# One value and one relative quarter of the products in each round; single maxima; first scores quad by quad

## The reference

```
Q, K, V = (layernorm(x) @ W.T + b) split into 16 heads of 8
rel_pos = arange(L)[None, :] - arange(L)[:, None] + 127      # clipped by the gather
scores  = einsum('bhld,bhrd->bhlr', Q, K) / sqrt(8) + einsum('bhld,lrd->bhlr', Q, relative_k[rel_pos])
attn    = softmax(scores)
out     = einsum('bhlr,bhrd->bhld', attn, V) + einsum('bhlr,lrd->bhld', attn, relative_v[rel_pos])
```

## Time and profile before

| | us |
|---|---|
| median of 3 runs | 2237.12 (2234.93 to 2237.24) |
| profiled execution, measured | 2237.36 |
| its span, first to last instruction | 2235.6 |
| PE busy | 2122.8 (95%) |
| DVE busy | 1701.9 (76%) |
| ACT busy | 1527.9 (68%) |
| POOL busy | 1059.3 (47%) |
| mean granted clock of TensorE | 0.991 |

### The profile page before, as it was taken

The page is one execution under the profiler, slowest core; times in us unless marked ns, Lnnn a source line. Parts: engine busy times, 40 slices in busy tenths (PEclk is TensorE's granted clock), DMA queues, the critical chain, the costliest instruction groups (busy, mean ns, idle before and its releaser), DMA issues.

```text
span 2235.6 us, 90813 instructions
## 1 busy us (share of the span) xinstructions
PE 2122.8 (95%) x37442; PEld 1549.0 (69%) x37442; DVE 1701.9 (76%) x3703; ACT 1527.9 (68%) x3290; POOL 1059.3 (47%) x992
## 2 busy tenths in 40 slices
PE   3999999999989999999899999999998999999998
PEld 1676766776667667676676676767776777777776
DVE  4788788888778888878688888788775676766675
ACT  3666666666666666666566666666664888888887
POOL 2443343344334433443343344434432777776776
PEclk8999999999999999999999999999998999999999
DMA  4112211321221122112212311222111222122110
GB/s 134 42 43 64 71 53 44 83 61 53 64 62 53 50 66 71 51 45 75 61 44 59 84 43 52 64 61 62 43 52 35 28 23 28 19 27 25 26 22 11
DMA packets 255701, 114.70 MB, mean 51 GB/s; under 512 B 142218, under 2 KB 251156, under 8 KB 255348
## 3 DMA queue, kind: packets, MB, share of 16 engines
q1 hardware_dynamic: 255348, 109.60, 20.2%
HBM read 83.34 MB, written 8.39 MB: 41 GB/s over the span
## 4 chain that ended last, share of the span: by engine, by line
PE 67%; DVE 12%; ACT 7%; issue 7%; POOL 3%; SPq 1%; DMA 0%; DVEq 0%; ACTq 0%; POOLq 0%
PE ps L1248 14%; PE ps L1187 9%; PE ps L1265 9%; PE ps L1194 7%; PE ps L1205 6%; PE ps L1277 5%; DVE neg_max L789 5%; POOL probs_t L500 3%; ACT probs L579 3%; ACT probs L646 2%; DVE probs_t L795 2%; PE ps L1431 2%; PE ps L1414 2%; PE ps L1416 2%; PE ps L1415 2%
## 5 line engine op out<-in xcount | busy, mean ns | idle before, releaser
L579 ACT ACTIVATE probs<-ps,neg_max 128x512 f32<-128x512 f32 x1024 | 695.0, 684 | 475.1 <-DVE neg_max L789 475.1
L789 DVE TENSOR_REDUCE neg_max<-ps 128x1 f32<-128x512 f32 (+1 forms) x768 | 619.5, 862 | 170.5 <-PE ps L1194 170.0
L439 POOL TENSOR_TENSOR stat_hi<-q_twice,mask8h 128x1024 f16<-128x1024 f16 x128 | 243.2, 1900 | 896.7 <-PE ps L1194 787.6
L1248 PE MATMUL ps<-const,probs 128*128 128x128 f32 x4096 | 516.3, 275 | 35.6 <-ACT probs L579 17.1
L1248 PEld LDWEIGHTS ps<-const,probs 128*128 128x128 f32 x4096 | 455.4, 142 | 89.1 <-issue 46.8
L795 DVE COPY probs_t<-ps 128x512 f32<-128x512 f32 x512 | 339.9, 685 | 88.7 <-PE ps L1248 84.5
L500 POOL TENSOR_TENSOR probs_t<-probs,probs_t 128x1024 f16<-128x1024 f32 x160 | 340.0, 2133 | 111.2 <-ACT probs_t L652 111.2
L568 ACT ACTIVATE probs_t<-ps 128x512 f32<-128x512 f32 x512 | 288.1, 596 | 98.2 <-PE ps L1248 94.7
L1187 PE MATMUL ps<-keys,stat_hi 128*32 128x512 f16 x4096 | 316.3, 384 | 1.8 <-issue 1.8
L1194 PE MATMUL ps<-rk_split,stat_rel 96*32 96x512 f16 (+1 forms) x4096 | 285.2, 353 | 0.0
L999 DVE SCALAR_TENSOR_TENSOR keys<-ps,comb,keys 128x128 f32<-128x128 f32 x640 | 179.8, 344 | 129.6 <-PE ps L1433 129.6
(11 more groups left out here) (136 smaller groups left out, 2870.2 us busy)
## 6 DMA issues: line engine op xcount, KB each, us to landing
rv_step<-in_rv_win SPq DMA_DIRECT2D x128, 512.0 KB, 3.9
keys<-keys SPq DMA_DIRECT2D x64, 96.0 KB, 2.2
x_pair<-in_x SPq DMA_DIRECT2D x8, 512.0 KB, 4.3
q_twice<-q_hi SPq DMA_DIRECT2D x32, 128.0 KB, 2.4
q_lo_pair<-q_lo SPq DMA_DIRECT2D x32, 128.0 KB, 2.8
rel_scratch<-rel_t SPq DMA_DIRECT2D x256, 16.0 KB, 3.2
x_pair<-in_x SPq DMA_DIRECT2D x16, 256.0 KB, 3.2
x_pair<-rel_scratch SPq DMA_DIRECT2D x64, 64.0 KB, 3.9
```

The lines of the kernel that those rows point to most:

```text
L579: nc.scalar.activation(probs[:, q, :], ps[:, i, :], ACT.Exp, bias=neg_max[:, q:q + 1], accum_out=row_sum[parity][:, s * QUADS + q:s * QUAD ...
L789: nc.vector.tensor_reduce(neg_max[:, IN_ROUND * j + at:IN_ROUND * j + at + n], ps[:, at:at + n, :], op=ALU.max, axis=AX_X, negate=True).th ...
L1248: last = nc.tensor.transpose(ps[:, bank, rt * P:(rt + 1) * P], probs[:, q, rt * P:(rt + 1) * P], ident)
```

## The change

Four things. Each of the four quads of a round gets its own reduce for the maximum, and every exponential waits for its own. In the steps 0 to 3, of the first two quads of each round, first terms and relative terms are issued quad by quad. Each round issues one batch of value products and one relative half, of step s - 2 (batch 1, half 1) in the first round and of step s - 1 (batch 0, half 0) in the second. The transposed relative rows go to the last quarter of the bank, and the wait for their copy (rel_t_ready) stands ahead of the value products of batch 1.

```diff
@@ -43,7 +43,6 @@
 
 ROUNDS = 2
 IN_ROUND = QUADS // ROUNDS
-MAXIMA = 3
 
 
 TR_BANKS = (0, 4, 5, 6)
@@ -574,8 +573,7 @@
                     act.wait_ge(tr_done, START + pair * TILES + (s - 1) * QUADS + IN_ROUND * (j + 1))
                 for i in range(IN_ROUND):
                     q = IN_ROUND * j + i
-                    if i < MAXIMA:
-                        act.wait_ge(max_done, START + ((pair * STEPS + s) * ROUNDS + j) * MAXIMA + i + 1)
+                    act.wait_ge(max_done, START + pair * TILES + s * QUADS + q + 1)
                     nc.scalar.activation(probs[:, q, :], ps[:, i, :], ACT.Exp, bias=neg_max[:, q:q + 1],
                                          accum_out=row_sum[parity][:, s * QUADS + q:s * QUADS + q + 1]).then_inc(exp_done, 1)
 
@@ -783,11 +781,10 @@
                                         rv_last_row[:].unsqueeze(1).broadcast_to([P, RT - FAR, D]), ALU.add).then_inc(operands_ready, 1)
 
             def maxima(pair, s, j):
-
-                for at, n in ((0, 1), (1, 1), (2, 2)):
-                    dve.wait_ge(score_done, START + pair * TILES + s * QUADS + IN_ROUND * j + at + n)
-                    nc.vector.tensor_reduce(neg_max[:, IN_ROUND * j + at:IN_ROUND * j + at + n], ps[:, at:at + n, :], op=ALU.max, axis=AX_X,
-                                            negate=True).then_inc(max_done, 1)
+                for i in range(IN_ROUND):
+                    q = IN_ROUND * j + i
+                    dve.wait_ge(score_done, START + pair * TILES + s * QUADS + q + 1)
+                    nc.vector.tensor_reduce(neg_max[:, q:q + 1], ps[:, i, :], op=ALU.max, axis=AX_X, negate=True).then_inc(max_done, 1)
 
             def evacuate(pair, s, q, piece):
 
@@ -824,7 +821,7 @@
                 dve.wait_ge(rel_tr, START + pair * STEPS + s + 1)
 
                 dve.wait_ge(rel_stored[s % 2], START + pair * STEPS * 16 + s // 2 * 32)
-                nc.vector.tensor_copy(rel_t[:, s % 2, :], ps[0:64, AV_BANK, 2 * P:3 * P]).then_inc(rel_t_ready, 1)
+                nc.vector.tensor_copy(rel_t[:, s % 2, :], ps[0:64, AV_BANK, 3 * P:4 * P]).then_inc(rel_t_ready, 1)
 
             def score_round(pair, parity, s, j, first, ahead):
                 maxima(pair, s, j)
@@ -1210,10 +1207,16 @@
                 for p in duos:
                     low_terms(parity, s, p)
                 for p in duos:
-                    for q in (2 * p, 2 * p + 1):
-                        first_terms(parity, s, q)
-                    for q in (2 * p, 2 * p + 1):
-                        relative_terms(s, q)
+                    if s < GROUP_STEPS and p % 2 == 0:
+
+                        for q in (2 * p, 2 * p + 1):
+                            first_terms(parity, s, q)
+                            relative_terms(s, q)
+                    else:
+                        for q in (2 * p, 2 * p + 1):
+                            first_terms(parity, s, q)
+                        for q in (2 * p, 2 * p + 1):
+                            relative_terms(s, q)
 
             def evacuated(pair, s, q):
 
@@ -1255,6 +1258,9 @@
                     evacuated(pair, s, QUADS - 1)
 
                     pe.wait_ge(rel_reduced, START + pair * STEPS + s)
+                else:
+
+                    pe.wait_ge(rel_t_ready, START + pair * STEPS + s)
                 if s == 0:
                     pe.wait_ge(operands_ready, START + pair * 6 + 5 + b)
                 for rt in range(RT):
@@ -1268,8 +1274,6 @@
             def relative_products(pair, s, half):
                 near = min(RT, s // GROUP_STEPS + FAR)
                 if half == 0:
-
-                    pe.wait_ge(rel_t_ready, START + pair * STEPS + s)
                     pe.wait_ge(rv_landed, START + (pair * STEPS + s + 1) * 16)
                 for rt in range(near):
                     for g in range(4):
@@ -1282,21 +1286,18 @@
             def rel_transposes(pair, s):
 
                 pe.wait_ge(rel_reduced, START + pair * STEPS + s + 1)
-                nc.tensor.transpose(ps[:, AV_BANK, 2 * P:3 * P], rel_o[:].rearrange("p a r -> p (a r)"), ident).then_inc(rel_tr, 1)
+                nc.tensor.transpose(ps[:, AV_BANK, 3 * P:4 * P], rel_o[:].rearrange("p a r -> p (a r)"), ident).then_inc(rel_tr, 1)
 
             def score_round(pair, parity, s, j, first, ahead):
                 scores(parity, s, j)
-                if j == 0:
-                    before, step = (pair, s - 2) if s >= 2 else (pair - 1, STEPS + s - 2)
-                    if s >= 2 or not first:
-                        for half in range(2):
-                            relative_products(before, step, half)
-                else:
-                    for b in range(2):
-                        if s:
-                            value_products(pair, s - 1, b)
-                        elif not first:
-                            value_products(pair - 1, STEPS - 1, b)
+
+                trailing = s - 2 + j
+                if trailing >= 0:
+                    value_products(pair, trailing, 1 - j)
+                    relative_products(pair, trailing, 1 - j)
+                elif not first:
+                    value_products(pair - 1, STEPS + trailing, 1 - j)
+                    relative_products(pair - 1, STEPS + trailing, 1 - j)
                 piece = piece_in(s, j, ahead)
                 if piece:
                     round_read(pair, s, j, 2)
@@ -1331,19 +1332,19 @@
 
             def last_step(pair):
                 s = STEPS - 1
-                for half in range(2):
-                    relative_products(pair, s - 1, half)
+                value_products(pair, s - 1, 1)
+                relative_products(pair, s - 1, 1)
                 transposes(pair, s, 1, False, None)
                 pe.wait_ge(spread_ready, START + 2)
                 evacuated(pair, s, IN_ROUND)
                 prepare_attention(0, 0, 0)
-                for b in range(2):
-                    value_products(pair, s, b)
+                value_products(pair, s, 0)
+                relative_products(pair, s, 0)
                 rel_transposes(pair, s - 1)
                 pe.wait_ge(ffn_loaded, 16 * FFN_LOADS)
                 prepare_output(0)
-                for half in range(2):
-                    relative_products(pair, s, half)
+                value_products(pair, s, 1)
+                relative_products(pair, s, 1)
                 prepare_h(0)
                 prepare_gates(0, 0)
                 rel_transposes(pair, s)
```

## The result

The changed kernel takes 2262.1 us (median of 5 runs, 2261.5 to 2264.6) against 2237.1: slower by 1.16%, ratio 1.0116 with a 95% interval of 1.0103 to 1.0129. The profiled execution took 2264.6, its span is 2262.8, 27.2 above the span before. Against the forecast of 2274 (2248 to 2294) it is 12 us faster.

What follows compares the result with a forecast made beforehand. PE, busy 95% of the span, was taken as the bound. Wait 42.6, restart 1, clock 19 and late windows 1, less a gain of 26.5, made +37 us: 2274 us, range 2248 to 2294.

Steps and rivals of the forecast that it cites:

- The wait: Step 14, second round: PE waits for the window queued behind query copies, seven times, mean 6.1 us: +42.6 us.
- the restart: PE starting again after each of the seven step 14 waits: 0.15 us x 7 = 1 us.
- The late ordinary windows: Ordinary steps: windows land with 0.7 to 1.2 us to spare, only rare long landings show: 1 us in all.
- The clock: After all seven step 14 waits PE falls to 1.2 GHz, 2.7 us each: +19 us, between 0 and 29.
- my price: Cost of a low clock, from two pair-edge rounds of 7.95 and 9.77 us against 5.63: +2.3 and +4.1.
- The gain: Shorter rounds from balanced products and earlier exponentials: 3.3 us a pair, 26.5 us in all.
- 17.1 us of waits: Transposes of L1248 waiting for exponentials before the change, read as showing how little there is to win.
- The sum: All terms together: +37 us on the profiled span of 2235.6; predicted time 2274.
- Rival 1: Step 14 stalls, but PE keeps its clock through 6 us: 2255 us; chance 13%.
- rival 2: Stall and clock, and DVE holds second rounds or quad order costs PE; gain about 10: 2290 us; chance 14%.
- rival 3: No late window in step 14, as SP finishes the query copies earlier: 2212 us; chance 4%.
- rival 4: Ordinary windows late too, some 100 steps x 0.3 = +30 us on top: 2304 us; chance 4%.

Runs made afterwards that it cites:

- e1: The changed kernel with step 13's value window issued ahead of the next pair's query copies in step 14: 2207.9 us, ratio 0.9867 to the kernel before.
- e2: The kernel before the change with the value window issued ahead of the query copies in step 14: 2237.0 us against 2235.5, ratio 1.0002.
- e3: The changed kernel with 48 identity transposes on PE just ahead of the late window wait: 2248.95 us, ratio 1.0058.
- e9: The kernel before the change with single maxima and nothing else: 2217.8 us, ratio 0.9917.
- e6: The kernel of e1 (window first) without the quad-by-quad order of scores in steps 0 to 3: 2207.5 us, ratio 0.9866.
- e4: The changed kernel with the products as before, leaving only single maxima and quad-by-quad scores: 2211.5 us, ratio 0.9892.
- e8: The changed kernel with step 13's value window issued behind the first of the four low-query copies: 2257.6 us, ratio 1.0084.

## Why the prediction was right, and where its sizes were off

*The wait.* Place, count and size as forecast: seven times, only in pairs with query copies, in the second round of step 14, 45.9 us less an eighth wait of 1.1. That is 44.7 for the seven, against 42.6 + 1 for the restart; PE also arrives 1.5 us earlier in all, which that step named and left out. e1 shows the cause, e2 that the order costs nothing without the new use.

*The late ordinary windows.* Forecast 1 us; the eighth wait, in the second round of pair 7's step 3, lengthened that round by 1.3 against its fellows. In e1 too, one wait of 1.0 us is all of it, so the spare time of an ordinary step held.

*The clock.* It fell at all seven, as forecast, but the term was mis-sized: 19 us predicted, 12.5 by the rounds (57.2 - 44.7), 13.1 by e3, so 1.8 or 1.9 a pair where I took 2.7. The fault lies in my price. I set the two disturbed rounds at a pair's edge, 7.95 and 9.77 us, against pair 4's 5.63, as if the clock were all that differed. In the changed kernel PE idled 3.46 us at the edge of pair 5 and the clock did not fall; here are that round's start and the round as a stretch.

```profile
1102.54 0.63 PE L1202 MATMUL ps<-keys,stat_lo 64*32 64x512 f16 x16 [3.46 <-issue]
```
```profile
1102.54:1109.69 7.15, 5.95 (x129) 4.42 (x130) 3.78 (x7) 3.23 (x9) 0.00 (x0) 1.00 0.08 15
```

Such a round takes 7.15 us at the full clock, with 1.2 us of idle in it; e9, whose products stand as in the kernel before, has one of 7.16 at 1.00 (first round of pair 3). So the low clock cost some 0.8 and 2.6 us in the earlier trace rows, not 2.3 and 4.1; the rest comes with the edge at any clock. A third such round, pair 3's in the changed kernel, took 7.15 at 0.79: there the clock cost nothing.

Why the price is below half of the slow time shows in these stretches of pair 3 in the changed kernel: the wait in two parts, then the work behind it.

```profile
861.82:864.96 3.14, 0.00 (x0) 0.00 (x0) 0.90 (x2) 1.93 (x6) 0.00 (x0) 1.00 0.64 147
864.96:867.94 2.98, 0.00 (x0) 0.00 (x0) 0.00 (x0) 0.00 (x0) 2.25 (x3) 0.54 0.68 189
867.94:871.79 3.85, 3.85 (x50) 3.34 (x51) 0.00 (x0) 0.86 (x1) 1.07 (x3) 0.50 0.00 0
871.79:874.70 2.91, 1.98 (x16) 1.68 (x15) 2.85 (x6) 0.76 (x2) 0.00 (x0) 0.96 0.01 3
```

The second part of the wait already stands at half clock, at no cost; only about 4 us were slow after it, and half of that, 2.0 us, is near what the rounds (12.5/7 = 1.8) and e3 (13.1/7 = 1.9) show per pair. The Trainium skill (TensorE: Matmul & The Clock Gate, HAM oscillation) counts half of all slow time. With 0.79 over 16.48 us, some 6.9 us slow, an estimate by that rule is 3.5 each, 24 in all; the measurement decides against it here, since slow time in which PE waits costs nothing. Nor do agree with it, as the prediction has it: some 2.6 us of the 9.77 were lost to the clock, where the rule gives 3.4.

*The gain.* Forecast 26.5. The other rounds gave 31.1, and 32.4 but for the eighth wait's 1.3; of this 3.4 are the first rounds of pairs 3 and 5, on which less of the low clock happened to fall, in pair 5 none (7.15 us in both against 7.95 and 9.77), which I count as chance, since these two rounds range from 6.9 to 9.8 us over the traces, and 1.5 the first rounds of step 14, which only moved into the wait. 27.5 are left. By rounds: 5.19 and 5.30 where I had 5.2 and 5.38; I had let DVE keep 0.08 us of the second round, and it kept none. 5.61 and 5.83 are as worked out. That the parts lean on each other I had not seen: by the ratios, the balance alone gives 8 us, the maxima alone 19, the maxima with the quad order 24, the balance with the quad order 17, the balance with the maxima 30, and all three 30 too. The prediction also began by calling 17.1 us of waits a sign of how little there is to win; that is less than what was won. From the kernel before to e1, PE's idle time falls by 18.8 us and its busy time by 9.5 (2122.8 to 2113.3); what the 9.5 are, this view does not tell.

*The sum.* On the span the forecast was +37.1 and the trace has +27.2: 6.5 less by the clock and 5.9 more gain (32.4 for 26.5), against 1.1 more wait, 0.3 more late windows and 1.2 at start and end. The two large misses point the same way and add up; 3.4 us of them are the chance at the pairs' edges.

*The rivals.* Rival 1 (no fall of the clock) is out by the granted clock; rival 2 (DVE eats the balance) by the full second rounds; rival 3 (faster, were the window early) is what e1 built: 2207.9 where that rival said 2212; rival 4 did not come.

## What to carry to other kernels

When a consumer moves earlier, walk the issuing queue around the producer in every step of the loop: in fifteen of sixteen steps this load came in time but for rare late landings, and the one where another job stood ahead of it turned a gain of 29 us into a loss of 25. Balancing an engine's work gains only down to the next chain in the same round; shorten the chain first (here the single maxima, some 19 us), then see what balance still adds (11 us on the single maxima, e9 to e6; on maxima and quad order together, e4 to e1, some 4 to 6, hardly clear of the noise). Price a fall of the clock by the work done slowly, not by the slow time, and against the same round at the full clock.

## What the runs showed of the hardware that I had not expected

A 512 KB load landed later with other copies issued behind it: in 5.9 to 6.9 us with three of 128 KB behind (e8), in 4.1 to 5.0 with four of 128 KB issued right behind it (e1), and in 3.9 to 4.3 with the 128 KB copies ahead of it and only two stores of 16 KB behind (the changed kernel). The last order is not safe from late landings: in e3 two of seven took 5.3 and 5.6 us.

Idle of PE at a pair's edge was followed by a fall of the clock in some traces and not in others: after 3.24 and 3.30 us it fell (the kernel before, pairs 3 and 5), after 3.46 us it did not (the changed kernel, pair 5). And 5.46 us of transposes of a constant held the clock at 1.00 through a 6 us wait and paid 13 us over seven waits (e3).
